# Value-bias term of the attention weights on VectorE instead of TensorE, attention sums taken earlier, and all box sums on VectorE

## The reference

```python
# 0: a 1x1 convolution whose weights are a sparsemax mix of 8 experts
g = sparsemax(pooled @ gate_w.T + gate_b)
w_eff = einsum('bk,koi->boi', g, expert_w)
# 1: depthwise 3x3, batch norm, relu, channels that stay below 4.0 set to 0, 1x1, batch norm, relu, prune
# 2: linear attention over the 784 pixels
qkv = xt @ Wqkv + bqkv            # q and k lose their mean over channels
k2n = k2 / (k2s + 1e-7); k2n = k2n / max(norm(k2n, over pixels), 1e-12)
q2n = q2 / (q2s + 1e-7); q2n = q2n / max(norm(q2n, over channels), 1e-12)
kv = einsum('bnc,bnd->bcd', k2n, v)
out = (v + einsum('bnc,bcd->bnd', q2n, kv) / sqrt(N)) @ Wln + bln
# 3: 3x3 box mean with zero padding
```

## Time and profile before

| what | value |
|---|---|
| median of 3 runs | 1684.85 us |
| lowest, highest | 1683.39, 1685.81 us |
| profiled execution | 1683.19 us, its span on the core 1681.4 us |
| busy in the span | PE 92%, DVE 86%, ACT 81%, POOL 25% |
| TensorE clock granted, mean | 0.972 |
| time from one step's `group_means` to the next, pipeline full | about 49 us |

### The profile page before, as it was taken

One profiled execution on the slowest core, in us unless ns is written; L12 is line 12 of the kernel. 1 busy time (PEld: TensorE's weight loads), 2 busy tenths in 40 slices (PEclk: granted clock), 3 DMA queues, 4 the chain that ended last, 5 costly groups with the idle time before them and its releaser, 6 DMA issues. The chain is left out here.

```text
span 1681.4 us, 26750 instructions
## 1 busy us (share of the span) xinstructions
PE 1543.4 (92%) x8190; PEld 1144.9 (68%) x8190; DVE 1452.5 (86%) x2530; ACT 1369.0 (81%) x3496; POOL 421.4 (25%) x269
## 2 busy tenths in 40 slices
PE   3569999999999999999999999999999999998994
PEld 2247777677777767777776777777677777766773
DVE  5867799999989999998999999899999989998646
ACT  3368988888888888888888888888888888878872
POOL 1111212233321223332122333212233321223224
PEclk8689999999999999999999999999999999999997
DMA  4000011100111110011111001111100111000000
GB/s 143 20 20 20 20 39 39 39 20 20 39 38 38 38 38 19 19 38 38 38 38 38 19 19 38 38 38 38 38 19 19 38 38 39 20 20 20 20 20 39
DMA packets 21058, 55.58 MB, mean 33 GB/s; under 512 B 2321, under 2 KB 3345, under 8 KB 21010
## 3 DMA queue, kind: packets, MB, share of 16 engines
q1 hardware_dynamic: 20914, 54.98, 9.3%
q10 hardware_dynamic: 96, 0.00, 0.0%
HBM read 29.29 MB, written 25.69 MB: 33 GB/s over the span
## 5 line engine op out<-in xcount | busy, mean ns | idle before, releaser
L769 DVE SCALAR_TENSOR_TENSOR h<-xpad,dw_sb,h 128x784 f32<-128x784 f32 x512 | 534.3, 1097 | 1.1
L540 PE MATMUL tile_ps<-wqk,xn_parts 128*112 128x512 f32 x1344 | 363.6, 425 | 0.0
L540 PEld LDWEIGHTS tile_ps<-wqk,xn_parts 128*112 128x112 f32 x1344 | 234.6, 175 | 80.2
L1223 POOL TENSOR_SCALAR xpad<-x,gn_r,gn_s 128x784 f32<-128x784 f32 x64 | 64.8, 1020 | 784.1 <-DVE gn_s L700 784.1
L448 PE MATMUL conv_ps<-h,pw_masked 128*128 128x392 f32 x512 | 183.5, 502 | 42.6 <-DVE x L805 37.1
L582 PE MATMUL tile_ps<-k,xT 112*128 112x256 f32 x896 | 205.1, 388 | 7.7 <-ACT xT L1029 7.7
L582 PEld LDWEIGHTS tile_ps<-k,xT 112*128 112x128 f32 x896 | 174.2, 195 | 40.1 <-issue 8.4
L963 ACT ACTIVATE junk<-x 128x784 bf16<-128x784 f32 x192 | 163.1, 851 | 40.6 <-DVE x L805 20.7
L570 PE MATMUL conv_ps<-x,mixed 128*128 128x392 f32 (+1 forms) x512 | 177.4, 499 | 2.2 <-ACT mixed L997 1.1
L448 PEld LDWEIGHTS conv_ps<-h,pw_masked 128*128 128x128 f32 x512 | 93.4, 192 | 111.6 <-DVE x L805 38.7
L448 PE MATMUL conv_ps<-xn_parts,w_out 128*128 128x392 f32 x768 | 153.1, 348 | 0.0
(11 more groups left out here) (143 smaller groups left out, 3020.5 us busy)
## 6 DMA issues: line engine op xcount, KB each, us to landing
x<-x SPq DMA_DIRECT2D x32, 784.0 KB, 4.3
out<-x SPq DMA_DIRECT2D x32, 784.0 KB, 3.5
expert_sb<-expert_rows SPq DMA_DIRECT2D x8, 256.0 KB, 5.5
x<-w_qk SPq DMA_DIRECT2D x1, 512.0 KB
x<-w_vT SPq DMA_DIRECT2D x1, 256.0 KB
x<-w_ln SPq DMA_DIRECT2D x1, 256.0 KB
pw_sb<-pw_wT SPq DMA_DIRECT2D x1, 256.0 KB
gmean<-group_mean SPq DMA_DIRECT2D x1, 64.0 KB, 4.0
```

The costliest lines, as they stand in the source:

```text
L540: mm = nc.tensor.matmul(bank, xn2_parts[:, u, i, m * TOK:(m + 1) * TOK], wqk[:, v, i, :], start=False, stop=(i == J - 1 and u == 1))
L769: ins = nc.vector.scalar_tensor_tensor(acc, view, scalar, acc, ALU.mult, ALU.add)
```

## The change

Four things are changed.

1. The bias matmuls of `attention_weights` go. `key_norms` on TensorE now turns both rows of `k_rows` into columns (four small matmuls, not two). ScalarE copies the totals to `k_total`, and VectorE adds `bv_ln` times the total to what it reads from PSUM, in a new function `attention_weights_sum`, into a buffer `attn_full` in SBUF. `attention_weights_high` and `_low` read `attn_full`.
2. VectorE's step: the new sums stand where the low parts were, the low parts follow the two `q_low`; `make_x3` comes right behind `x2_low`, `h_mask` ahead of the box sums, and seven depthwise turns in one piece behind them. The turns alternate between the halves with no offset.
3. The box sums of both halves are done on VectorE, in four instructions of twice the width; GpSimd has none.
4. `sparsemax` has two instructions fewer and one wait fewer.

```diff
-                for c in range(J):
-                    mm = nc.tensor.matmul(tile_ps[:, KSUM_BANK, c:c + 1], k_rows[:, 1, half(c)], ones[:, 0:1], start=True,
-                                          stop=True, skip_group_check=True)
+                for n in range(2):
+                    for c in range(J):
+                        mm = nc.tensor.matmul(tile_ps[:, KSUM_BANK, n * J + c:n * J + c + 1], k_rows[:, n, half(c)],
+                                              ones[:, 0:1], start=True, stop=True, skip_group_check=True)
...
                 pe.wait_ge(kx_lo.sem, kx_lo.at(E))
-                pe.wait_ge(ksum_read.sem, ksum_read.at(E))
                 for c in range(J):
                     dst = tile_ps[:, ATTN_BANK, c * C:(c + 1) * C]
-                    nc.tensor.matmul(dst, k_rows[:, 0, half(c)], bv_ln[:], start=True, stop=False)
...
+            def attention_weights_sum(E):
+
+                dve.wait_ge(knorm_read.sem, knorm_read.at(E, 1))
+                dve.wait_ge(attn_w_mm.sem, attn_w_mm.at(E))
+                for c in range(J):
+                    nc.vector.scalar_tensor_tensor(attn_full[:, c, :], bv_ln[:], k_total[:, c:c + 1],
+                                                   tile_ps[:, ATTN_BANK, c * C:(c + 1) * C], ALU.mult,
+                                                   ALU.add).then_inc(attn_sum.sem, 1)
...
             def attention_weights_low(E):
-                dve.wait_ge(attn_hi.sem, attn_hi.at(E))
                 for c in range(J):
-                    nc.vector.scalar_tensor_tensor(attn_parts[:, 1, c, :], tile_ps[:, ATTN_BANK, c * C:(c + 1) * C],
+                    dve.wait_ge(attn_hi.sem, attn_hi.at(E, c + 1))
+                    nc.vector.scalar_tensor_tensor(attn_parts[:, 1, c, :], attn_full[:, c, :],
                                                    k_inv[:, 1, c:c + 1], attn_parts[:, 0, c, :].bitcast(F32),
                                                    ALU.mult, ALU.subtract).then_inc(attn_lo.sem, 1)
...
                 if E.active:
+                    attention_weights_sum(E)
+                    q_low(E, range(2, 4))
                     attention_weights_low(E)
-                    q_low(E, range(2, 4))
                 if A.active:
                     sparsemax(A)
...
                 if D.active:
                     x2_low(D)
-                if B.active:
-                    depthwise(B, slice(1, 3))
-                if F.active:
-                    box_sums(F, range(BOX_STEPS))
-                if C_.active:
-                    h_mask(C_)
-                if B.active:
-                    depthwise(B, slice(3, 5))
                 if E.active:
                     make_x3(E)
                 if B.active:
-                    depthwise(B, slice(5, 9))
+                    depthwise(B, slice(1, 3))
+                if C_.active:
+                    h_mask(C_)
+                if F.active:
+                    box_sums(F, range(BOX_STEPS))
                 if B.active:
-                    depthwise(B, slice(9, 10))
+                    depthwise(B, slice(3, 10))
                 if D.active:
                     reciprocal_sums(D)
...
             def attention_weights_high(E):
-                act.wait_ge(attn_w_mm.sem, attn_w_mm.at(E))
                 act.wait_ge(kinv_step.sem, kinv_step.at(E))
+                if (E - 1).active:
+                    act.wait_ge(attn_mm.sem, attn_mm.at(E - 1))
                 for c in range(J):
-                    nc.scalar.activation(attn_parts[:, 0, c, :], tile_ps[:, ATTN_BANK, c * C:(c + 1) * C],
-                                         ACT.Identity, scale=k_inv[:, 1, c:c + 1]).then_inc(attn_hi.sem, 1)
+                    act.wait_ge(attn_sum.sem, attn_sum.at(E, c + 1))
+                    nc.scalar.activation(attn_parts[:, 0, c, :], attn_full[:, c, :], ACT.Identity, scale=k_inv[:, 1, c:c + 1]).then_inc(attn_hi.sem, 1)
...
-                for n in range(BOX_STEPS):
-                    if n:
-                        pool.wait_ge(box_step[1].sem, box_step[1].at(F, n))
-                    nc.gpsimd.tensor_tensor(*box_operands(1, n), ALU.add).then_inc(box_step[1].sem, 1)
```

More of the change, by code:

```diff
@@ L29 @@
 PACKED = EXPERTS // STRIPS
-GATE_STEPS = 17
+GATE_STEPS = 15
 XW = HW + 2
@@ L137, in build @@
         ones = sb("ones", [P, P])
+        zeros = sb("zeros", [P, 1])
         ones16 = sb("ones16", [P, TOK], BF16)
@@ L193, in build @@
         tau = sb("tau", [P, 4])
-        gate = sb("gate", [P, 2, EXPERTS])
+        gate = sb("gate", [P, EXPERTS])
         gate_own = sb("gate_own", [P, PACKED])
@@ L211, in build @@
         k_rows = sb("k_rows", [P, 2, C])
+        k_total = sb("k_total", [P, J])
+        attn_full = sb("attn_full", [P, J, C])
         conv_ps = ctx.enter_context(nc.psum_tensor("conv_ps", [P, 4, 512], F32))
@@ L290, in build @@
         x3pad_ready = sig("x3pad_ready", J)
-        box_step = [sig(f"box_step{j}", BOX_STEPS) for j in range(J)]
+        box_step = sig("box_step", BOX_STEPS)
         x4_ready = sig("x4_ready", J)
@@ L302, in split, with box_operands @@
             return tile.rearrange("p (a n) -> p a n", a=2)
[L304 to L312, removed]
+        def box_operands(n):
+            inner = x3pad[:, :, 1:1 + H, 1:1 + W]
+            sums = row_sums[:, :, 1:1 + H, :]
+            return [(sums, x3pad[:, :, 1:1 + H, 0:W], inner),
+                    (sums, sums, x3pad[:, :, 1:1 + H, 2:2 + W]),
+                    (inner, row_sums[:, :, 0:H, :], sums),
+                    (inner, inner, row_sums[:, :, 2:2 + H, :])][n]
         def conv_banks(j):
@@ L332, in build @@
         QUADS = [(j, ms) for j in range(J) for ms in ([0, 1, 2, 3], [4, 5, 6])]
-        TAP_TURNS = [(0, 0)] + [turn for n in range(1, TAPS) for turn in ((0, n), (1, n - 1))] + [(1, TAPS - 1)]
+        TAP_TURNS = [(j, n) for n in range(TAPS) for j in range(J)]
         block = ctx.enter_context(nc.Block())
@@ L459, in q_to_channels @@
                 pe.wait_ge(qa_ready.sem, qa_ready.at(E))
-                before = [[], [(E, knorm_read, 1)], [(E, qT_lo, 1)], [(E, qT_lo, 2)]]
+                before = [[], [(E, knorm_read, 2)], [(E, qT_lo, 1)], [(E, qT_lo, 2)]]
                 for n in banks:
@@ L500, in attention_weights @@
                 pe.wait_ge(kx_lo.sem, kx_lo.at(E))
-                pe.wait_ge(ksum_read.sem, ksum_read.at(E))
                 for c in range(J):
                     dst = tile_ps[:, ATTN_BANK, c * C:(c + 1) * C]
-                    nc.tensor.matmul(dst, k_rows[:, 0, half(c)], bv_ln[:], start=True, stop=False)
                     for i in range(J):
                         for u, v in ((0, 0), (0, 1), (1, 0)):
-                            mm = nc.tensor.matmul(dst, kx_parts[:, u, i, half(c)], w_out[:, v, i, :], start=False,
-                                                  stop=(i == J - 1 and u == 1))
+                            mm = nc.tensor.matmul(dst, kx_parts[:, u, i, half(c)], w_out[:, v, i, :],
+                                                  start=(i == 0 and u == v == 0), stop=(i == J - 1 and u == 1))
                 mm.then_inc(attn_w_mm.sem, 1)
@@ L531, in queries_keys @@
                 pe.wait_ge(xn2_lo.sem, xn2_lo.at(D))
-                before = [[(D - 1, qT_lo, 3)], [(D - 1, qT_lo, 4)], [(D - 1, attn_lo, J)]
+                before = [[(D - 1, qT_lo, 3)], [(D - 1, qT_lo, 4)], [(D - 1, attn_sum, J)]
                           ] + [[(D, k2_ready, m - 2)] for m in range(3, M)]
@@ L1041, in key_norms @@
                 act.wait_ge(knorm_mm.sem, knorm_mm.at(E))
-                nc.scalar.activation(k_norm[:], tile_ps[:, KSUM_BANK, 0:J], ACT.Sqrt, scale=1.0 / SUB).then_inc(knorm_read.sem, 1)
+                if (E - 1).active:
+                    act.wait_ge(attn_sum.sem, attn_sum.at(E - 1))
+                nc.scalar.copy(k_total[:], tile_ps[:, KSUM_BANK, 0:J]).then_inc(knorm_read.sem, 1)
+                nc.scalar.activation(k_norm[:], tile_ps[:, KSUM_BANK, J:2 * J], ACT.Sqrt, scale=1.0 / SUB).then_inc(knorm_read.sem, 1)
             def fourth_powers(D):
@@ L1250, in step @@
                     normalise_x1(A, B, C_)
-                if F.active:
-                    box_sums(F)
                 if C_.active:
@@ L1262 @@
 SETUP_DVE = SETUP_BN + 10 + 2 + 2 + 2
-SETUP_POOL = 9
+SETUP_POOL = 10
 QT_BANK, KSUM_BANK, ATTN_BANK = [0, 2, 0, 2], 2, 1
```

45 lines of the change are left out of this document (23 added, 22 removed).

## The result

The changed kernel took 1665.35 us (median of 4 runs, 1664.32 to 1665.90) against 1685.07 us of the kernel before (4 runs). The ratio is 0.9884, with a 95% interval of 0.9867 to 0.9901. That is 1.2% less; the prediction said 1668. The kernel before ran 22 more times beside the experiments, 12 of them between 1683.7 and 1685.8 us like these four and 10 between 1678.0 and 1682.0, so the gain is 1.2% against most of its runs and about 0.8% against the others.

What follows compares the result with a forecast made beforehand. A chain through several engines, not one full engine, was taken to set the step: 8.87 + 39.46 = 48.33 us against 49.06. 27 x -0.73 = -19.7, plus 3.9 outside full steps, gave -15.8 and 1668 us, range 1652 to 1688.

Steps and rivals of the forecast that it cites:

- The two halves of the step: From `key_rows` to `attention_out`, forecast 8.87 us, and from there to the next `key_rows`, forecast 39.46 us.
- What bounds the kernel: No engine is full; a chain through several sets the step, and late VectorE costs TensorE most of 2.4 us a step.
- The attention path: From `key_rows` to `attention_out`: forecast 1.27 us longer than the 7.60 before, with nothing on TensorE able to cover it.
- The price of the masks: GpSimd's mask pair beside VectorE's box sums: forecast to cost them 0.35 us a step, bounds 0 and 0.94.
- the pair at 850.12: GpSimd mask pair in the kernel before that cost the turns beside it nothing; cited for the bound of 0.
- The lock rival: Mask pair blocks VectorE's box sums for all its time, 0.94 us: step 48.92, 1685 us, no change; chance 0.13.
- The wait ahead of `attention_out`: New TensorE wait for the low parts of the weights: forecast about 1.5 us a time, some 27 times.
- Outside the full steps: Early steps, those after A ends and the program's end: forecast +5.2 - 1.3 = +3.9 us in all.
- The round trip: Hand-overs between VectorE and ScalarE dearer, attention path 0.9 us longer: step 49.23, 1693 us, slower; chance 0.12.
- The box stage isn't the limit: GpSimd costs nothing there, wide sums run a little better: step 47.8, 1655 us; chance 0.14.
- TensorE becomes the limit: Both TensorE waits go, step 46.7 us or less, time 1621 us; needs an attention path no longer; chance 0.03.
- The end of the program: Attention first, then F's double box sums (7.2) and `make_x4` (1.8): statistics +3.7 us; very last step -1.5.

Runs made afterwards that it cites:

- e3: Kernel before with only the box sums changed, all on VectorE in four double-width instructions at the old place: 1615.27 us, ratio 0.9591.
- e1: Changed kernel with the bias matmuls back on TensorE and the weights' low parts ahead of the queries' on VectorE: 1626.31 us, ratio 0.9663 to the kernel before.
- e2: Kernel before with only the bias term moved from TensorE to VectorE, its sums ahead of the query parts: 1708.66 us, ratio 1.0149.
- e6: Changed kernel with one swap on ScalarE, the second pair's query high parts ahead of those of the attention weights: 1629.63 us, ratio 0.9683 to the kernel before.
- e5: Changed kernel with each of GpSimd's two mask products done twice, the extra into its own buffer: 1677.71 us, ratio 0.9972 to the kernel before.
- e8: Changed kernel with GpSimd's two mask products replaced by constant fills, leaving the multiplication out: 1655.95 us, ratio 0.9841 to the kernel before.
- e4: Kernel before with only VectorE's new order, GpSimd keeping its half of the box sums: 1651.22 us, ratio 0.9812.

## Why the prediction was right

| term, us | predicted | measured |
|---|---|---|
| `key_rows` to `attention_out` | 8.87 | 872.79 - 863.83 = 8.96 |
| `attention_out` to `h_mask` | 8.30 | 881.11 - 872.79 = 8.32 |
| four box sums with the masks beside them | 7.2 + 0.35 | 888.70 - 881.19 = 7.51 |
| seven turns | 6.6 | 895.32 - 888.70 = 6.62 |
| copies of tokens to the next `key_rows` | 16.27 | 912.14 - 895.88 = 16.26 |
| `attention_out` to the next `key_rows` | 39.46 | 912.14 - 872.79 = 39.35 |
| full step, mean of 27 | 48.33 | 48.26 |

The two halves of the step miss by +0.09 and -0.11 us, and that they cancel is luck; neither is large.

*What bounds the kernel.* A chain through VectorE and ScalarE with TensorE waiting: right, and e3 shows the other end of it, where the chain is short and TensorE sets the step with 46.73.

*The attention path.* Longer by 1.36 us instead of 1.27. e1 and e2 show that it costs, e6 shows why. The reading that it can't be covered held for the order as written; the swap covers most of it.

*The price of the masks.* 0.35 was taken from turns in an early step. The sums lost 0.15 each in two of four, about 0.3. The bounds of 0 and 0.94 were wide, and the nearer row was the right one. Why the pair at 850.12 in the kernel before cost the turns beside it nothing stays open. The lock rival, 0.94, is out by e5 and e8.

*The wait ahead of `attention_out`.* Forecast at 1.5 us, measured 1.30. The difference is mostly a new short wait of TensorE ahead of the second transposes, 5.6 us in 24 times, which the sum had not listed. It only takes its 0.2 us out of the longer wait behind it.

*Outside the full steps.* Forecast +3.9, and the spans differ by 1663.7 - 1681.4 = -17.7 = 27 x -0.80 + 3.9. This agreement is partly chance. By the `group_means` of both traces, the start up to the first full step gives +0.2 where -0.5 was forecast; the two steps after A ends give +1.8 against +1.5; the one after that -0.4 against +0.7; the end +2.3 against +2.2. The shorter `sparsemax` brought 8.2 us of waiting instead of 9.2, 0.34 a step instead of 0.44: part of the rest is its last instruction, which grew from 0.22 to 0.28 with a third operand. Two steps moved with TensorE's clock, below.

*The rivals.* The round trip was dearer by 0.09, not by 0.9. "The box stage isn't the limit" needed masks at no cost and a little more. e8 grants the first: 47.97 a step, which is the forecast less its 0.35, and not yet that rival's 47.8. "TensorE becomes the limit" was reached only with the attention path short.

*The end of the program* came as laid out: `make_x3` before the box sums, which now stand alone. VectorE:

```profile
1637.29 1.04 DVE L808 SCALAR_TENSOR_TENSOR x<-conv_ps,b_out,x 128x784 f32<-128x784 f32 x1 [1.04 <-PE conv_ps L452]
...
1638.25 1.79 DVE L821 TENSOR_TENSOR row_sums<-x3pad 128x1568 f32<-128x1568 f32 x1
...
1647.33 0.17 DVE L689 COPY gn_avg<-small_ps 128x16 f32<-128x16 f32 x1
```

The next statistics come 1647.33 - 1637.29 = 10.0 us after the second `make_x3` begins; before, 1663.60 - 1659.88 = 3.7 us after the first of the pair.

## What to carry to other kernels

A wait that vanishes says little: follow the chain once around the step, from an instant to the same instant a step later, with durations of rows, and compare the two sums. When an edit makes one engine wait for another that waited for the first, look at what stands behind the new wait in the queue, and put work there that depends on neither; here one swapped pair of lines was worth 1.1 us a step. Before sharing an elementwise stage between VectorE and GpSimd, compare a row of VectorE beside GpSimd's reads with one without: here four sums of twice the width alone took as long as four of single width in company, and the neighbours ran freely.

## What the runs showed of the hardware that was not expected

A product on GpSimd and a sum on VectorE that both read SBUF don't share the cost evenly. Beside GpSimd's products a double-width sum goes from 1.79 to 1.95 us, while GpSimd's pair takes 3.74 us where it took 0.94 when free. Each product ends 0.34 or 0.35 us after the end of a sum (e5), while the sum takes only 0.15 us more. Beside GpSimd's sums, which read two operands, a turn of VectorE takes 2.18 instead of 0.95, a product of one operand 2.24 instead of 0.62, and one of two columns 1.71 instead of 0.17 (e4).

TensorE's granted clock moved two single steps, and no term had them. Third step from the end, the last part of it in the kernel before and in the changed one (busy us of PE, PEld, DVE, ACT, POOL, granted clock, DMA share, GB/s):

```profile
1626.00:1643.00 17.00, 13.68 (x74) 10.04 (x72) 2.89 (x8) 13.14 (x39) 0.00 (x0) 0.80 0.12 48
```

```profile
1606.00:1623.00 17.00, 13.68 (x79) 10.03 (x78) 2.89 (x8) 13.90 (x42) 0.00 (x0) 0.90 0.12 48
```

The mean of 0.80 before and 0.90 after lies between the two levels of 1.2 and 2.4 GHz (0.5 and 1.0 in these rows): the engine spent less of this stretch at the lower one. In both it had waited twice for ScalarE's copies just before (1.84 and 1.42 us, then 1.85 and 1.42), and the 28 matmuls of `keys_x` took 9.20 and 7.97 us. In an early step it went the other way: the first tile of `queries_keys` took 2.58 us after and 1.79 before, and that step is 0.45 us longer. What made the clock rise sooner or later there was not tried and stays open.
